# A transformer block on one core: a new order of the small jobs, one PSUM bank moved from row maxima to jobs, and the score band as the stationary operand

## What is computed

```python
h = _layernorm(x) * (1 + ca) + sa
x = x + ga * attn(h)          # 16 heads of 16 columns
h = _layernorm(x) * (1 + cb) + sb
x = x + gb * ffn(h)

# attn: scores = (q / 4) @ k.T + 8 * rel_bias[bucket(mem - ctx)], softmax over 512 keys
# bucket: max(ctx - mem, 0), exact under 16, logarithmic up to 64, then constant (31)
# ffn: every operand is rounded to blockwise FP4 (blocks of 16, scale = max|x| / 6)
gate, y = fp4_linear(x, w_gate), fp4_linear(x, w_up)
return fp4_linear(silu(gate) * y, w_down)      # 704 hidden columns
```

## Time and profile before

| | us |
|---|---|
| runs: median (3 runs, lowest to highest) | 3641.7 (3631.09 to 3645.46) |
| the profiled execution's own time | 3629.85 |
| its span, first to last instruction | 3628.0 |
| PE busy | 3295.2 (91%) |
| DVE busy | 2916.0 (80%) |
| ACT busy | 2121.1 (58%) |
| POOL busy | 1709.8 (47%) |

### The profile page before, as it was taken

The page is one execution under the profiler, slowest core; times in us unless marked ns, Lnnn a source line. Parts: engine busy times, 40 slices in busy tenths (PEclk is TensorE's granted clock), DMA queues, the critical chain, the costliest instruction groups (busy, mean ns, idle before and its releaser), DMA issues.

```text
span 3628.0 us, 78368 instructions
## 1 busy us (share of the span) xinstructions
PE 3295.2 (91%) x20870; PEld 1926.6 (53%) x20870; DVE 2916.0 (80%) x9982; ACT 2121.1 (58%) x3351; POOL 1709.8 (47%) x2098
## 2 busy tenths in 40 slices
PE   5799999999999999999999999999999999999985
PEld 2345555555555555555555555555555555555554
DVE  6878888888888888888888888887888888888855
ACT  2466566666655665655666665666565666566552
POOL 2325454544454544444544444544444544445454
PEclk7899999999999999999999999999999999999997
DMA  8342333232333333334323234323244323233000
GB/s 191 59 80 56 74 75 75 60 63 57 64 75 76 65 58 60 58 76 76 68 62 57 55 75 77 70 58 60 52 76 77 72 57 59 53 75 72 20 20 12
DMA packets 200281, 238.33 MB, mean 66 GB/s; under 512 B 23600, under 2 KB 178640, under 8 KB 199808
## 3 DMA queue, kind: packets, MB, share of 16 engines
q1 hardware_dynamic: 199840, 233.08, 33.0%
HBM read 163.59 MB, written 67.31 MB: 64 GB/s over the span
## 4 chain that ended last, share of the span: by engine, by line
issue 48%; POOL 31%; PE 11%; DVE 3%; ACT 3%; POOLq 2%; DMA 1%; SPq 0%; ACTq 0%; DVEq 0%
POOL hidden L1332 4%; POOL hidden L1330 4%; POOL hidden L1359 4%; PE ps_x L675 4%; POOL parts L1296 3%; POOL proj L1289 3%; POOL ffn_in L1347 2%; POOL rstd L1342 2%; PE rings L630 2%; POOL x_mid L1325 2%; PE ps_o L664 2%; PE rings L646 1%; POOL hidden L1334 1%; POOLq L124 1%; ACT probs L818 1%
## 5 line engine op out<-in xcount | busy, mean ns | idle before, releaser
L1070 DVE CUSTOM_DVE_ANT_0 rings<-rings,band_z 128x512 f32<-128x512 f32 x2048 | 1407.9, 698 | 164.7 <-issue 163.7
L818 ACT ACTIVATE probs<-rings 128x1024 f32<-128x1024 f32 x1024 | 1049.5, 1025 | 720.0 <-PE rings L633 711.6
L630 PE MATMUL rings<-q_rows,k_rows 121*128 121x512 bf16 x2048 | 729.7, 384 | 77.9 <-ACT probs L818 62.8
L646 PE MATMUL rings<-k_rows,q_rows 120*128 120x512 bf16 x2048 | 768.9, 387 | 27.7 <-DVE row_max L1070 26.2
L664 PE MATMUL ps_o<-probs,values 128*32 128x512 f32 x4096 | 550.6, 610 | 0.9 <-ACT probs L818 0.9
L646 PEld LDWEIGHTS rings<-k_rows,q_rows 120*128 120x128 bf16 x2048 | 191.9, 97 | 510.7 <-DVE row_max L1070 270.6
L631 PE MATMUL rings<-band_t,rev 128*128 128x128 f16 x2048 | 451.0, 220 | 0.0
L1359 POOL TENSOR_TENSOR hidden<-hidden,inv 128x704 f32<-128x704 f32 x128 | 178.5, 1394 | 545.7 <-DVE inv L1109 545.7
L633 PE MATMUL rings<-band_t,rev 128*128 128x128 f16 (+1 forms) x2048 | 431.9, 211 | 0.0
L675 PE MATMUL ps_x<-w_gu_h,xq_h 128*128 128x512 f32 (+1 forms) x768 | 350.8, 457 | 19.5 <-DVE hq_l L1123 17.2
L633 PEld LDWEIGHTS rings<-band_t,rev 128*128 128x128 f16 x2048 | 201.8, 99 | 247.8 <-issue 3.2
(11 more groups left out here) (187 smaller groups left out, 6923.1 us busy)
## 6 DMA issues: line engine op xcount, KB each, us to landing
parts_dram<-parts SPq DMA_DIRECT2D x128, 384.0 KB, 2.4
q_rows<-parts_dram SPq DMA_DIRECT2D x384, 128.0 KB, 4.3
k_rows<-parts_dram SPq DMA_DIRECT2D x384, 128.0 KB, 7.2
mod_rows<-mod_rows_dram SPq DMA_DIRECT2D x32, 640.0 KB, 5.6
x_in<-in_x SPq DMA_DIRECT2D x32, 512.0 KB, 8.4
x_mid<-in_x SPq DMA_DIRECT2D x128, 128.0 KB, 2.0
out<-x_mid SPq DMA_DIRECT2D x128, 128.0 KB, 1.7
probs<-in_wmod SPq DMA_DIRECT2D x1, 1536.0 KB, 6.9
```

What stands on the lines that cost most here:

```text
L630: mm(ps_s[:, bank, :], kr[0:ROW_MAX + 1, h, k0:k0 + P], qr[0:ROW_MAX + 1, h, :], start=True, stop=False)
L646: mm(ps_m[:, bank, :], q_rows[par][0:ROW_MAX, h, j * P:(j + 1) * P], k_rows[par][0:ROW_MAX, h, :], start=True, stop=True).then_inc(mscores ...
L818: A(prob_pair(s, j), ps_s, ACT.Exp).then_inc(exp_done, 1)
L1070: v.tensor_tensor_reduce(ps, ps, band_z[:, bias:bias + S], 1.0, LOWEST, ALU.add, ALU.max, row_max[:, par, 4 * h + j:4 * h + j + 1]).then_i ...
```

## The change

1. **Order of the jobs.** g2 moves from (2, 2) to (2, 0), hT0 and hT1 from (2, 0) and (2, 1) to (2, 2) and (2, 3), down from (3, 1) to (3, 2); the batch's jobs move too, and the values are now three jobs. `add_ffn` moves from (3, 3) to (0, 0) and (0, 3) of the next group. `magic3` is computed at (3, 1) and (3, 3) of the group before, in place of (0, 0).
2. **Banks.** Jobs use three banks in turn, maxima two.
3. **Band.** `band_t` is widened to 256 columns and becomes the stationary operand; the moving one is the first 64 columns of `rev`. A score gets three such matmuls (two for the last block of keys).
4. **Set-up.** The weights' power of two comes from ScalarE's Square and Identity, and GpSimd adds and subtracts it; the weights' block scales are computed at the end of iteration -2. One table copy per pair of heads in place of two. The tile `exp2` is gone; its place is taken by the second half of `tanh` (`gated`), with waits for it.

```diff
-RING_S, RING_M = 2, 3
+RING_S, RING_M, RING_X = 2, 2, 3
...
     group = {(0, 0): "ctxT", (0, 1): "xqT", (0, 3): "wo", (1, 0): "g0", (1, 2): "oT", (1, 3): "g1",
-             (2, 0): "hT0", (2, 1): "hT1", (2, 2): "g2", (3, 1): "down"}
-    batch = {(1, 1): "v0", (2, 3): "v1", (3, 2): "m1", (5, 1): "xT0", (6, 3): "xT1", (7, 2): "p0", (7, 3): "p1",
-             (10, 3): "p2", (11, 2): "p3", (12, 2): "m0"}
+             (2, 0): "g2", (2, 2): "hT0", (2, 3): "hT1", (3, 2): "down"}
+    batch = {(0, 2): "v0", (2, 1): "m1", (3, 0): "v1", (4, 2): "v2", (5, 1): "xT0", (6, 1): "xT1", (7, 0): "p0",
+             (8, 2): "p1", (10, 1): "m0", (11, 0): "p2", (12, 2): "p3"}
...
-            t, _, k = JOBS[at - 2]
-            return (self.n - 1 if at < 2 else self.n), t, k
+            t, _, k = JOBS[at - RING_X]
+            return (self.n - 1 if at < RING_X else self.n), t, k
...
-        band_t = sb("band_t", [P, H, P], F16)
+        band_t = sb("band_t", [P, H, 2 * P], F16)
...
-                mm(ps_s[:, bank, k0:k0 + P], rev[:, 0, :], band_t[:, h, :], start=False, stop=False)
-                w = min(P, S - k0 - HALF)
-                mm(ps_s[:, bank, k0 + HALF:k0 + HALF + w], rev[:, 1, :], band_t[:, h, 0:w],
-                   start=False, stop=True).then_inc(scores_ready, 1)
+                windows = 3 if kb < NT - 1 else 2
+                for w in range(windows):
+                    m = mm(ps_s[:, bank, k0 + w * HALF:k0 + (w + 1) * HALF],
+                           band_t[:, h, P - w * HALF:2 * P - w * HALF], rev[:, 0, 0:HALF], start=False, stop=w == windows - 1)
+                m.then_inc(scores_ready, 1)
...
-                        if (r, j) == (0, 0) and it.has_tile(s, 2):
-                            u = it.tile(s, 2)
+                        if (r, j) == (3, 1) and it.has_tile(s, 1):
+                            u = it.tile(s, 1)
                             after(act, f2_pool, u, "xn")
                             after(act, f3_pool, u - 1, "sub")
-                            A(magic3[:], hidden[:, (g + 1) % 2, :], ACT.Square, scale=ROOT).then_inc(f3_act.sem, 1)
-                            after(act, f3_act, u, "sq")
+                            A(magic3[:], hidden[:, g % 2, :], ACT.Square, scale=ROOT).then_inc(f3_act.sem, 1)
+                        if (r, j) == (3, 3) and it.has_tile(s, 1):
+                            after(act, f3_act, it.tile(s, 1), "sq")
                             A(magic3[:], magic3[:], ACT.Identity, bias=floor[:]).then_inc(f3_act.sem, 1)
...
-                if stage == 2:
-                    after(dve, w_pool, 0, f"div{k}")
-                    wstep(v.tensor_scalar(e.bitcast(I32), w.bitcast(I32), EXPONENT, None, ALU.bitwise_and), f"exp{k}")
-                    wstep(v.tensor_scalar(e, e, 1.0, MAGIC, ALU.max, ALU.mult), f"magic{k}")
-                    wstep(v.tensor_tensor(w, w, e, ALU.add), f"add{k}")
-                    wstep(v.tensor_tensor(w, w, e, ALU.subtract), f"round{k}")
...
-                        if at == (3, 3) and it.has_tile(s, 2):
-                            add_ffn(it, s)
+                        if at in ((0, 0), (0, 3)) and it.has_tile(s, 3):
+                            add_ffn(it, s, j // 3)
...
-                            if at == (3, 0):
+                            if at == (2, 2):
                                 after(dve, f2_dve, u, "h2")
                                 after(dve, f3_pool, u - 1, "q")
                                 block_scales(f2_dve, u, scale3[:], inv3[:], hid)
...
-                    if r == 3 and it.has_tile(s, 1):
+                    if r == 2 and it.has_tile(s, 1):
                         hid = hidden[:, g % 2, :]
                         after(pool, f2_dve, it.tile(s, 1), "inv")
```

More of the change, by code:

```diff
@@ L157, in batch_of @@
         return n + 2
-    if kind in ("v0", "v1", "m0"):
+    if kind in ("v0", "v1", "v2", "m0"):
         return n + 1
@@ L168, in tile_of @@
     return n * NT + (s // 4 - 1 - lag - NT)
-WEIGHT_SPOTS = ((8, "ctxT"), (8, "xqT"), (8, "wo"), (9, "g0"), (9, "g1"), (10, "hT0"), (10, "hT1"), (10, "g2"),
+WEIGHT_SPOTS = ((8, "ctxT"), (8, "xqT"), (8, "wo"), (9, "g0"), (9, "g1"), (10, "g2"), (10, "hT0"), (10, "hT1"),
                 (12, "ctxT"), (12, "xqT"), (13, "g0"))
@@ L209, in fresh, with earlier @@
         return Iteration(eng.snap(copy, min_val=LOOP[0] // 2, max_val=LOOP[1] // 2 - 1), self.par, True)
+    def earlier(self, s):
+        if s:
+            return self
+        return Iteration(self.pair - 1 + self.par, 1 - self.par, self.steady)
     def has(self, shift):
@@ L418, in build @@
         inv_w = [flat(x_mid)[:, scale_at[3] + scale_at[k]:scale_at[3] + scale_at[k + 1]] for k in range(3)]
-        w_exp = w_setup[:, 2 * DT * FF:4 * DT * FF]
+        w_exp = w_setup[:, 2 * DT * FF:4 * DT * FF].bitcast(BF16)
+        w_magic = [w_exp[:, FT * D * k:FT * D * k + w_nat[k].shape[1]] for k in range(3)]
         CR = slice(ROWS_QK, P)
@@ L681, in job @@
                 number, bank = it.job(s, kind)
-                before = it.two_before(s, kind)
+                before = it.ring_before(s, kind)
                 if before:
@@ L706, in job @@
                     after(pe, a_act, n + 1, "h1b")
-                    for k in range(2):
-                        tt = 2 * int(kind[1]) + k
+                    for k in range(2 if kind == "v1" else 1):
+                        tt = (0, 1, 3)[int(kind[1])] + k
                         for dt in range(DT):
@@ L1305, in emit @@
                     rp = 1 - par if s >= 4 else par
-                    if not it.steady and n == 0:
-                        weights(s)
+                    if not it.steady and n in (-1, 0):
+                        weights(n, s)
                     if s == 4 and it.has(2):
```

185 lines of the change are left out of this document (93 added, 92 removed).

## The result

| | before | after |
|---|---|---|
| median of the runs, us | 3636.39 | 3416.96 |
| lowest to highest | 3630.32 to 3645.46 | 3416.14 to 3429.22 (4 runs) |
| the profiled execution | 3629.85 | 3417.14 |
| its span | 3628.0 | 3415.2 |
| PE, DVE busy | 3295.2, 2916.0 | 3166.1, 2832.6 |

The account below looks back on a forecast made before the run. The prediction took TensorE's queue to set the pace, VectorE 19 us per batch behind; -61 - 105 - 37 - 41 + 70 - 10 = -184 from the profiled 3629.85 gave 3446 us, the forecast's own range 3370 to 3530, overall 3330 to 3590.

Parts of the forecast that it names:

- Band, -61: TensorE's band matmuls: 0.03 us saved on each of 2048 scores, all in the queue that bounds, 61 us less.
- the rival of the loads: Weight loads bind: each 64-column band matmul holds TensorE 0.06 us, band +108 us, 3615 us in all; chance 0.02.
- Jobs' waits, -105: TensorE's waits for VectorE before jobs, for operand or bank: three quarters of 140 us go, 105 us less.
- Scores' waits, -37: TensorE's waits before scores, for ScalarE's exponentials or no named event: half of 75 us goes, 37 us less.
- The hidden part, -41: Some eight TensorE waits per batch go, each worth 0.16 us more than its idle time: 41 us less.
- Two banks, +70: Maxima with one bank less wait for VectorE's reductions, at (2, 1) to (3, 1): 70 us more.
- Set-up, -10: Start of the kernel: rounding and block scales of weights cheaper, wider band table 9 us dearer; together 10 us less.
- VectorE's adds, 0: VectorE's adds of two SBUF tiles beside GpSimd's: the moved one slowed, the attention's freed, set against each other at 0.
- The first rival: Jobs' gains are eaten by waits for maxima's banks and ScalarE; only band and set-up remain: 3559 us, chance 0.17.

Follow-up runs that it names:

- e1: The kernel before with only the band's matmuls in the new form, three of 64 columns per score, table not widened: 3636.8 us, ratio 1.000.
- e5: The changed kernel with the two 128-column band matmuls of before in place of three of 64 columns: 3441.0 us, ratio 0.946.
- e3: The kernel before, old order, with both bank changes: three banks for jobs, two for maxima: 3618.2 us, ratio 0.995.
- e6: The changed kernel with the banks of before (three for maxima, two for jobs) and the values in two jobs again: 3552.4 us, ratio 0.977.
- e12: The changed kernel with x loaded half a batch earlier and the loop over pairs of batches written out: 3322.6 us, ratio 0.915.
- e7: The changed kernel with the load of the next x tile started half a batch earlier: 3367.2 us, ratio 0.926.
- e2: The kernel before with two banks for maxima in place of three, jobs keeping two: 3672.9 us, ratio 1.010.
- e8: The kernel before with the rounding constant `magic3` moved behind the jobs' copies at (0, 0), behind `ctx_h` but ahead of `xq_h`: 3608.5 us, ratio 0.993.
- e9: The kernel before with `magic3` behind the jobs' copies at (0, 0) and the 64-column band matmuls, table not widened: 3598.9 us, ratio 0.991.

## Why the prediction was right, and where it was not

The time, 3417, lies 29 us under the forecast and within its range; the direction held, and so did the mechanism of the jobs' waits, with corrections below. Per batch, 6.5 us went. The stream gave 1.6. TensorE's idle time fell from 166.5 us in 22.1 batches (7.5 each) to 109.3 in 23.6 (4.6 each): 2.9. Its waits fell from 285 to 82 in 2400 us, 12.9 to 3.5 per batch, and at the forecast's 0.16 us hidden in each, which no run tests apart, that is 1.5. 0.5 us is left over. The lower clock works against the sum: 34.1 us of it in place of 13.7 in the 2400, at most 0.4 us a batch, so up to 0.9 stay without a name. This ledger says where the time went; the runs say that its entries aren't independent.

- **Band, -61.** The price of an instance was nearly right, 0.025 us for 0.03, 50 in all. The step that failed is "since all of it lies in the queue that bounds": alone it gave 0 (e1), in the new order 24 (e5). TensorE was busiest, but a batch's length hung on its waits. Three full loads with 64-column matmuls start within 0.06 us (0.25 less 0.19, L638), so the rival of the loads has fallen. The Trainium skill, page "TensorE: Matmul & The Clock Gate", section "Back-to-back issue gap", states some 81 ns for a load and matmul of 128 columns in a sustained stream, by which the band would have become dearer. In this case's pairs they start 0.06 us apart (1830.35, 1830.41 in the earlier trace rows), so the trace does not agree.
- **Jobs' waits, -105.** All of it went, 105.1 us to 0.0: 4.75 per batch with the groups that the sum had left out, 152 in 32. "The rest stays because hT1 and `hq_l` are now close to `down`" was wrong. But neither banks nor order does it usefully alone: with banks alone it comes back at the maxima (e3), with the order alone 109.3 us remain (e6).
- **Scores' waits, -37.** The exponentials' part went further than half, 38.5 to 9.4 us. Not seen was the other part: the waits for instructions nearly doubled, 13.4 to 25.5, and without the loop they are gone (e12). Together 2.34 to 1.77 per batch, -18.
- **The hidden part, -41.** 9.4 waits fewer per batch and not 8: -48 by the same 0.16.
- **Two banks, +70.** 9.5 to 67.5 us, 0.43 to 2.86 per batch: +78. The size is right, and that is partly luck. It was forecast for (2, 1) to (3, 1) of each group, behind the block scales and `hq_l`. Half of it (34.2 us) stands there, but in the last group of a batch alone, and stays in e7 and e12 (35.4 each). The other half (30.6 us) stands at slot 3 behind the load of x, a wait that the forecast didn't price, and is gone in e7.
- **Set-up, -10.** 0. The first batch gave 23.0 us, as the forecast had it within a few (16 and some 8). But the first exponential comes 23.2 us later, where 9 were allowed for the wider table; which step of the new set-up takes them was not tested.
- **VectorE's adds, 0.** The two x_mid adds took 1493 + 668 ns in the mean, now 1059 + 819, 0.28 us less per tile; what that is worth no run shows. The Trainium skill, page "GPSIMD Engine Reference", section "Key points", says that GpSimd shares its SBUF interfaces with VectorE and contends with instructions of two SBUF inputs. The trace agrees in the direction: the attention's add became shorter, the moved one longer, though the first is far from free of it (425 ns is its shortest).

```profile
L1148 DVE TENSOR_TENSOR x_mid<-tanh,x_mid 128x256 f32<-128x256 f32 x94 | 99.6, 1059 | 3.4
...
L1196 DVE TENSOR_TENSOR x_mid<-tanh,x_mid 128x256 f32<-128x256 f32 x94 | 77.0, 819 | 0.0
```
```profile
L1138 DVE TENSOR_TENSOR x_mid<-exp,x_mid 128x256 f32<-128x256 f32 x89 | 132.9, 1493 | 3.0
L1198 DVE TENSOR_TENSOR x_mid<-exp,x_mid 128x256 f32<-128x256 f32 x89 | 59.5, 668 | 3.0
```

The first rival, waits that change place, is what e1, e2, e3, e8 and e9 show for every single part in the old order; it fell only for the whole. That the forecast's sum of separate prices came out near is partly luck: the band's 61 (50 of stream, 24 when taken out alone), the scores' 37 and the set-up's 10 were too much, the jobs' 105 too little. What exactly holds a batch of the old order at 108 us is left open. Taking away the jobs' waits (e3) or some of TensorE's work (e1), or moving VectorE's wait to another copy (e8), changed it by under 1 us each. The test that is missing is the old order with the constant a slot earlier, as in the change, so that neither `ctx_h` nor `xq_h` stands behind it.

## What to carry to other kernels

The busiest engine at 91% need not be the pace: before a shorter stream is priced in full, ask whether the waits behind it end at the same releases as before, and price it in the order in which it will run. On engines that work in order, moving one operation from ahead of the copy that everyone waits for was worth 97 us in the new order, more than the 24 of the leaner matmuls; moved by one copy only, it made the wait change place (e8). A bank is worth only what the order can use (18 us alone, 135 in the new order). When the queues fit, look at what is left in each turn: one load issued half a batch late cost 50 us, and the turns of a loop 45. Look at the granted clock beside the idle time, since a wait can cost more than it lasts. And measure a start by a step that kept its place: by the copies that moved, the set-up seems to give 9 us, by the exponentials nothing.
